# Two graph layers on one core: the second layer's probabilities turned by the transposing DMA instead of TensorE

## What is computed

```python
# layer 0
h = jnp.einsum('bnd,ade->bane', feat_in, W); th = jnp.tanh(h)
attn = attn_src + jnp.swapaxes(attn_dst, 2, 3)          # from th, leaky, masked, softmax
feat_out = jax.nn.elu(einsum(attn, h) + b)
gate = jax.nn.sigmoid(feat_in @ H_w.T + H_b)
l0 = gate * feat_out + (1.0 - gate) * feat_in
x = _layernorm(x + l0)
# layer 1: 6 heads of 128
q, k, v = _heads(x @ Wq + bq), _heads(x @ Wk + bk), _heads(x @ Wv + bv)
probs = softmax(q @ k.T / sqrt(128) + bias, axis=-1)    # 64 x 64 for each graph and head
x = _layernorm(x + (probs @ v) @ Wf + bf)
```

## Time and profile before

| | before |
|---|---|
| median of 3 runs | 2766.53 us (2765.67 to 2773.51) |
| profiled execution: its own time | 2766.33 us |
| its span, first to last instruction | 2764.6 us |
| PE busy | 99% |
| DVE, ACT, POOL busy | 60%, 42%, 39% |
| mean granted clock of PE | 0.997 |

### The profile page before, as it was taken

One profiled execution on the slowest core, in us unless ns is written; L12 is line 12 of the kernel. 1 busy time (PEld: TensorE's weight loads), 2 busy tenths in 40 slices (PEclk: granted clock), 3 DMA queues, 4 the chain that ended last, 5 costly groups with the idle time before them and its releaser, 6 DMA issues.

```text
span 2764.6 us, 51821 instructions
## 1 busy us (share of the span) xinstructions
PE 2726.9 (99%) x20988; PEld 2517.8 (91%) x20988; DVE 1668.8 (60%) x3334; ACT 1160.3 (42%) x3045; POOL 1066.3 (39%) x630
## 2 busy tenths in 40 slices
PE   8999999999999989999999999999999999999998
PEld 6877778888788889999999999999999999999998
DVE  6888998888888754444454444454445445444443
ACT  5666776666666633322332233322332233223322
POOL 2453344433444134433444343434443343434340
PEclk9999999999999999999999999999999999999999
DMA  5656665555555512222213222222222222222220
GB/s 180 173 131 145 164 160 145 139 139 139 141 137 143 175 59 69 69 71 81 70 58 81 76 75 58 79 72 71 69 68 71 81 70 58 81 81 70 58 70 23
DMA packets 306894, 269.49 MB, mean 97 GB/s; under 512 B 227808, under 2 KB 244192, under 8 KB 306656
## 3 DMA queue, kind: packets, MB, share of 16 engines
q1 hardware_dynamic: 306656, 266.19, 35.5%
HBM read 142.65 MB, written 75.89 MB: 79 GB/s over the span
## 4 chain that ended last, share of the span: by engine, by line
PE 85%; DVE 5%; DMA 4%; issue 2%; POOL 2%; ACT 2%; SPq 1%; DVEq 0%; ACTq 0%; POOLq 0%
PE ps_hg L1036 21%; PE ps_a L1199 14%; PE ps_k L70 14%; PE ps_q L70 14%; PE ps_a L70 14%; PE ps_c L1165 2%; PE ps_s L1140 2%; PE ps_pv L1068 1%; DMA dst_all<-dst_scratch 1%; ACT logits L564 1%; PE ps_t L1055 1%; PE ps_pt L1165 1%; DMA dst_scratch<-dst 1%; PE ps_pt L1147 1%; DVE logits L770 1%
## 5 line engine op out<-in xcount | busy, mean ns | idle before, releaser
L1036 PE MATMUL ps_hg<-w_hi,xT 128*128 128x512 f32 x2268 | 745.6, 401 | 8.3 <-DVE h_one L803 8.2
L1036 PEld LDWEIGHTS ps_hg<-w_hi,xT 128*128 128x128 f32 x2268 | 426.1, 188 | 112.6 <-issue 11.3
L1036 PE MATMUL ps_hg<-w_lo,xT 128*128 128x512 f32 x1134 | 448.4, 395 | 0.0
L70 PE MATMUL ps_k<-x1T_hi,wk_hi 128*128 128x256 f32 x1152 | 329.1, 286 | 0.0
L70 PE MATMUL ps_q<-x1T_hi,wq_hi 128*128 128x256 f32 x1152 | 323.5, 281 | 1.4 <-DVE x1T_lo L910 1.4
L70 PE MATMUL ps_q<-x1T_lo,wq_hi 128*128 128x256 f32 x1152 | 322.6, 280 | 0.0
L70 PE MATMUL ps_k<-x1T_lo,wk_hi 128*128 128x256 f32 x1152 | 321.9, 279 | 0.0
L70 PE MATMUL ps_q<-x1T_hi,wq_lo 128*128 128x256 f32 x1152 | 321.9, 279 | 0.0
L70 PE MATMUL ps_k<-x1T_hi,wk_lo 128*128 128x256 f32 x1152 | 321.1, 279 | 0.0
L496 POOL TENSOR_TENSOR th_src<-th,wsrc_all 128x768 f32<-128x768 f32 x64 | 118.3, 1848 | 483.7 <-DVE dst_all L783 463.4
L648 ACT ACTIVATE qT<-ps_q,bq_col 128x256 f32<-128x256 f32 x192 | 80.5, 470 | 479.3 <-PE ps_q L70 479.3
(11 more groups left out here) (144 smaller groups left out, 5814.2 us busy)
## 6 DMA issues: line engine op xcount, KB each, us to landing
x_tok<-x SPq DMA_DIRECT2D x64, 384.0 KB, 4.1
dst_all<-dst_scratch SPq DMA_DIRECT2D x128, 192.0 KB, 3.4
gate_scratch<-gate SPq DMA_DIRECT2D x64, 384.0 KB, 2.6
feat_scratch<-feat SPq DMA_DIRECT2D x128, 192.0 KB, 2.8
feat_in<-feat_scratch SPq DMA_DIRECT2D x62, 384.0 KB, 3.1
gate_in<-gate_scratch SPq DMA_DIRECT2D x62, 384.0 KB, 3.7
x_even<-x SPq DMA_DIRECT2D x16, 768.0 KB, 4.2
x_odd<-x SPq DMA_DIRECT2D x16, 768.0 KB, 4.4
```

The source lines that it names most:

```text
L70: ins = pe.matmul(out, left[a][c], right[b][c], start=(n == 0), stop=(n == len(terms) - 1))
L1036: ins = pe.matmul(ps_hg[:, cols], left[a][c], right[b][c], start=(c == 0 and n == 0), stop=(c == KC - 1 and n == 2))
```

## The change

From group 2 on PE no longer turns the probabilities. POOL splits `scores_sb` into two planes of 16 bits (`split_p1`), SP issues one transposing DMA of four 128x128 blocks (`turn_p1`), and the copies into `probs1T` now read the turned planes and join them (`join_block`). For the first two pairs ACT joins the blocks of tile 0 and DVE those of tile 1; for the third pair ACT joins all four. `scores` gets a wait for the logits of the pair before, which the transposes had implied. `scores_sb` is free for the next logits when POOL has split it. SP issues the three turns of a group after the second tile's feat and gate loads and ahead of the next group's `turn_x1`.

Besides, for all groups and for the first part too, the gate is completed on ACT (`whole_gate`, 0.5 times plus 0.5) where POOL added 1, with the constants of the mix and of its epsilon changed to suit. On DVE, `rstd_start` of the next group's input stands ahead of the third pair's logits, the second pair's joins behind them, and `rstd_end` ahead of the third `normalise`.

```diff
+        def join_block(copy, buf, t, g, signal):
+            s = graph(g)
+            out_ = probs1T[s, buf, :, s].bitcast(U16).rearrange("p (h t) (n l) -> p l h t n", t=GT, l=2)[:, :, :, t, :]
+            copy(out_, planes_p1T[t * NODES:(t + 1) * NODES, :, :, s]).then_inc(signal, 1)
...
+            def turn_p1(G, j):
+                sp.wait_ge(split_p1_done, pair_of(G, j))
+                for joined_ in (block0_done, block1_done):
+                    sp.wait_ge(joined_, 2 * (PAIRS * G + j))
+                sp.dma_start_transpose(planes_p1T.rearrange("p l h n -> p (l h) n"),
+                                       planes_p1.rearrange("p l (h m) -> p (l h) m", h=2)).then_inc(turned_p1, 16)
...
+                if G + 2 < NG:
                     sp.wait_ge(mixed, GT * (G + 2) + 1)
                     feat_and_gate(G + 2, 1)
+                if BY_DMA <= G + 1 < NG:
+                    for j in range(PAIRS):
+                        turn_p1(G + 1, j)
...
                 pool.wait_ge(delta_done, GT * G + t + 1)
-                pool.tensor_scalar(gate_, gate_, 1.0, None, ALU.add).then_inc(gate_ready, 1)
                 pool.wait_ge(gate_ready, GT * G + t + 1)
...
+            def split_p1(G, j):
+                pool.wait_ge(probs_done, PAIRS * G + j + 1)
+                if pair_of(G, j) > 1:
+                    pool.wait_ge(turned_p1, 16 * (pair_of(G, j) - 1))
+                pool.tensor_copy(planes_p1[:, :, :], scores_sb.rearrange("p k m -> p (k m)").bitcast(U16)
+                                 .rearrange("p (d l) -> p l d", l=2)).then_inc(split_p1_done, 1)
...
-                for t in range(GT):
+                for t in range(GT):
+                    if 1 <= G < NG - 1:
                         feat_less_x(G + 1, t, feat_in[:, :])
                         times_gate(G + 1, t, feat_in[:, :], gate_in[:, :])
+                    if G >= BY_DMA:
+                        split_p1(G, t)
+                if G >= BY_DMA:
+                    split_p1(G, GT)
...
+            def whole_gate(G, t, gate_):
+                if G == 0:
+                    act.wait_ge(fg_first[t], 32)
+                else:
+                    act.wait_ge(fg_in, 32 * (GT * (G - 1) + t + 1))
+                act.activation(gate_, gate_, ACT.Copy, scale=0.5, bias=0.5).then_inc(gate_ready, 1)
...
                 if G == 0:
                     for n in range(KC + 3, 2 * KC):
                         w1_round(act, EARLY_W1 + n)
+                    whole_gate(1, 1, gate_in[:, :])
...
             def scores(G, j):
+                if G >= BY_DMA:
+                    pe.wait_ge(logit_done, PAIRS * G + j)
...
-                transpose_probs1(G, 0)
+                if G < BY_DMA:
+                    transpose_probs1(G, 0)
                 scores(G, 1)
```

More of the change, by code:

```diff
@@ L195, in two_graph_layers @@
         bf_all = at(S + 55232, "bf_all", [P, D])
+        planes_p1 = at(S + 53184, "planes_p1", [P, 2, PN * NODES], U16)
+        planes_p1T = at(S + 54208, "planes_p1T", [P, 2, 2, P], U16)
         x1_tok = [x_even, x_odd]
@@ L244, in two_graph_layers @@
         turned1 = [sem(f"turned1_{t}") for t in range(GT)]
+        split_p1_done, turned_p1 = (sem(n) for n in ("split_p1_done", "turned_p1"))
         v_done, v_copied, o_done, o_added = (sem(n) for n in ("v_done", "v_copied", "o_done", "o_added"))
@@ L249, in two_graph_layers @@
             sem(n) for n in ("bias_mask", "logit_done", "max1_done", "exp1_done", "inv1_done", "probs_done"))
-        pt1_done, ptc_act, ptc_dve, c_done, c_hi, c_lo = (
-            sem(n) for n in ("pt1_done", "ptc_act", "ptc_dve", "c_done", "c_hi", "c_lo"))
+        pt1_done, block0_done, block1_done, c_done, c_hi, c_lo = (
+            sem(n) for n in ("pt1_done", "block0_done", "block1_done", "c_done", "c_hi", "c_lo"))
         biased, stat_done, mv_done, newton, norm_done = (
@@ L264, in copy_block, with pair_of @@
             copy(out_, src_).then_inc(signal, 1)
+        def join_block(copy, buf, t, g, signal):
+            s = graph(g)
+            out_ = probs1T[s, buf, :, s].bitcast(U16).rearrange("p (h t) (n l) -> p l h t n", t=GT, l=2)[:, :, :, t, :]
+            copy(out_, planes_p1T[t * NODES:(t + 1) * NODES, :, :, s]).then_inc(signal, 1)
+        def pair_of(G, j):
+            return PAIRS * (G - BY_DMA) + j + 1
         def turn_of(G, t):
@@ L629, in _ @@
                     elu_exp(T - 2)
+                for t in range(GT):
+                    if T == MIX + 2 * t:
+                        whole_gate(0, t, gate_first[:, t, :])
                 if PREFETCH < T <= PREFETCH + EARLY_W1 - LATE_W1:
@@ L677, in probs_out @@
             def probs_out(G, j):
-                act.wait_ge(pt1_done, PAIRS * G + j + 1)
-                for g in range(2):
-                    copy_block(act.copy, (G + j) % 2, 0, g, ptc_act)
+                if G < BY_DMA:
+                    act.wait_ge(pt1_done, PAIRS * G + j + 1)
+                    for g in range(2):
+                        copy_block(act.copy, (G + j) % 2, 0, g, block0_done)
+                else:
+                    act.wait_ge(turned_p1, 16 * pair_of(G, j))
+                    for g in range(2):
+                        join_block(act.copy, (G + j) % 2, 0, g, block0_done)
+                    if j == PAIRS - 1:
+                        for g in range(2):
+                            join_block(act.copy, (G + j) % 2, 1, g, block1_done)
             def context_hi(G, j):
@@ L708, in _ @@
                     k_out(G, 0)
+                    if G + 1 < NG:
+                        whole_gate(G + 1, 0, gate_in[:, :])
                 q_out(G, 1)
                 exps(G, 0)
+                if G == 0:
+                    whole_gate(1, 0, gate_in[:, :])
                 k_out(G, 1)
                 q_out(G, 2)
+                if 1 <= G < NG - 1:
+                    whole_gate(G + 1, 1, gate_in[:, :])
                 if G == 0:
@@ L724, in _ @@
                 value_out(G, 0)
-                probs_out(G, 1)
+                if G < BY_DMA:
+                    probs_out(G, 1)
                 exps(G, 2)
+                if G >= BY_DMA:
+                    probs_out(G, 1)
                 value_out(G, 1)
@@ L895, in _ @@
                     input_moments(0)
-                    rstd_start(in_newton, 0, 4 * EPS)
+                    rstd_start(in_newton, 0, EPS)
                 elif T == MIX + 2 * GT + 2:
@@ L916, in logits_of @@
                     dve.wait_ge(bias_mask, G + 1)
+                elif G < BY_DMA:
+                    dve.wait_ge(pt1_done, PAIRS * G + j)
                 else:
-                    dve.wait_ge(pt1_done, PAIRS * G + j)
+                    dve.wait_ge(split_p1_done, pair_of(G, j - 1))
                 dve.scalar_tensor_tensor(
@@ L934, in probs_out @@
             def probs_out(G, j):
-                dve.wait_ge(pt1_done, PAIRS * G + j + 1)
-                for g in range(2):
-                    copy_block(dve.tensor_copy, (G + j) % 2, 1, g, ptc_dve)
+                if G < BY_DMA:
+                    dve.wait_ge(pt1_done, PAIRS * G + j + 1)
+                    for g in range(2):
+                        copy_block(dve.tensor_copy, (G + j) % 2, 1, g, block1_done)
+                else:
+                    dve.wait_ge(turned_p1, 16 * pair_of(G, j))
+                    for g in range(2):
+                        join_block(dve.tensor_copy, (G + j) % 2, 1, g, block1_done)
             def context_lo(G, j):
@@ L975, in _ @@
                     input_moments(G + 1)
-                probs_out(G, 1)
+                    if G >= BY_DMA:
+                        rstd_start(in_newton, G + 1, EPS)
+                if G < BY_DMA:
+                    probs_out(G, 1)
                 logits_of(G, 2)
-                if 1 <= G < NG - 1:
-                    rstd_start(in_newton, G + 1, 4 * EPS)
+                if G >= BY_DMA:
+                    probs_out(G, 1)
+                elif G >= 1:
+                    rstd_start(in_newton, G + 1, EPS)
+                if BY_DMA <= G < NG - 1:
+                    rstd_end(in_newton, G + 1)
                 normalise(G, 2)
@@ L983, in _ @@
                     input_moments(1)
-                    rstd_start(in_newton, 1, 4 * EPS)
+                    rstd_start(in_newton, 1, EPS)
+                if G < BY_DMA:
+                    rstd_end(in_newton, G + 1)
                 if G + 1 < NG:
-                    rstd_end(in_newton, G + 1)
                     input_norm(G + 1)
                 context_lo(G, 0)
-                probs_out(G, 2)
+                if G < BY_DMA:
+                    probs_out(G, 2)
                 if G == 0:
@@ L1168, in probs_copied @@
             def probs_copied(G, j):
-                pe.wait_ge(ptc_act, 2 * (PAIRS * G + j + 1))
-                pe.wait_ge(ptc_dve, 2 * (PAIRS * G + j + 1))
+                pe.wait_ge(block0_done, 2 * (PAIRS * G + j + 1))
+                pe.wait_ge(block1_done, 2 * (PAIRS * G + j + 1))
             def first_context(G):
```

(6 more changed lines are left out.)

3 lines of the change are left out of this document (1 added, 2 removed).

## The result

The changed kernel is slower: median 2783.94 us (2780.21 to 2785.95, 6 runs) against 2767.48 us (6 runs), ratio 1.0051, 95% interval 1.0040 to 1.0061. The forecast was 2752 us, 2747 to 2762. The profiled execution took 2785.95 us, its span is 2784.2 us.

What follows compares the result with a forecast made beforehand. PE, busy 99% of the span, was taken to bound the kernel: 2766.33 - 17.7 saved by PE + 3.3 lost in group 0 = 2751.9, forecast 2752 us, range 2747 to 2762; the new chain was to cost nothing.

Steps and rivals of the forecast that it cites:

- what PE saves: PE without transposes in groups 2 to 31: 0.59 us less a group, 17.7 us in all, bounds 13.5 and 22.8.
- group 0: Gate completed on ACT behind three casts delays group 1's normalised x, which PE awaits: +3.3 us, bounds 0 and 3.6.
- the turn, by itself: Transposing DMA of four probability blocks: lands in 3.0 us, between 2.2 and 4.0.
- The 5.2 us: Turn of four blocks, if the skill's 1309 ns by DMA added up one after another: an estimated 5.2 us.
- a pair of joins ... I take 0.84: Copies joining a pair's turned planes into `probs1T`: 0.84 us, from ACT passes of 256 elements.
- they can be about 1 us later than before: Second pair's logits on DVE, behind the first pair's joins: about 1 us later than before.
- the very mechanism, for `normalise`: First pair's normalise on DVE meets POOL's product over the shared port: up to 0.6 us more.
- the prediction's chain: DVE, POOL, DMA and joins up to the third pair: ready at 1897.0 to 1898.6, PE asks at 1899.9, 1.3 us left.
- the split: POOL's split of `scores_sb` into two planes: about 0.6 us with its start.
- ACT's four joins: Third pair's four joins on ACT: 1.6 us.
- the place of the slack: Third pair taken as the tight one: its blocks ready 1.3 us before PE asks, 0.3 with slow turn and chain.
- The rival on the other side: Third pair late in every group through split, turn and four joins in a row: 27 us, 2779 us; chance 0.07.

Runs made afterwards that it cites:

- experiment 7: Kernel before the change, with only the gate completed on ACT and probabilities still turned by TensorE: 2765.34 us, ratio 0.9991.
- experiment 9: Changed kernel, but SP issues a group's first turn ahead of the second tile's feat and gate loads: 2751.93 us, ratio 0.9942.
- experiment 6: Changed kernel, but POOL waits for DVE's join of the first pair before subtracting x from the second tile's feat: 2755.02 us, ratio 0.9959.
- experiment 1: Changed kernel, but DVE computes the second pair's logits before joining the first pair's blocks: 2754.32 us, ratio 0.995.
- experiment 2: Changed kernel, but ACT joins all four blocks of the first pair and DVE none: 2754.01 us, ratio 0.9951.
- kernel 5: Changed kernel with DVE's second-pair logits ahead of its first-pair joins, and group 0's second gate ahead of ACT's casts: 2750.84 us, ratio 0.9941.

## Why the prediction was wrong

**Right: what PE saves.** I put 0.59 us a group and 17.7 us; measured 0.66 and 19.8. The difference may be the third pair, whose transposes may cost more than their starts; no run tests it.

**Right in its mechanism, unsettled in size: group 0.** PE's wait for `x_odd` rose by 3.6 us as worked out. The term was +3.3 us; group 0 got longer by 0.8 to 3.1 (experiment 7), and experiment 7 shows the gate part as a whole at -1.3 us (0 to -5 by its interval). In it is some 1.8 us of lost time of late groups, which went.

**Right: the turn, by itself.** I took 3.0 us; four blocks land in 2.4 (median of 90), with 4.0 still that of twelve:

```profile
DMA to landing us min/median/max: 2.4/2.4/7.0
```

The upper end is that of the first turns, which go behind the loads: they take 4.0 us in the median, and only ahead of the loads (experiment 9) 2.4. The place still came out: the first turn lands 23.4 us after the start of the group shown, where I put 22.0 to 23.5. The 5.2 us, estimated from the 1309 ns that the Trainium skill (VectorE: DVE Perf Modes, the three transpose paths) gives for one 128x128 block by DMA, are not borne out as a sum of blocks.

**Wrong: the step "a pair of joins ... I take 0.84", and with it "they can be about 1 us later than before".** For the first pair on DVE the joins take 3.5 us (median), and the second pair's logits start 3.8 us later than before. The estimate came from ACT's passes and ACT's old copies, which read PSUM; the new copies have SBUF on both sides, and on DVE they stand at the time of POOL's subtraction and product. Two paragraphs below that step the prediction tells of the very mechanism, for `normalise`, and draws on the Trainium skill (SBUF — State Buffer) for operations with two SBUF inputs. In the section "Who interferes with whom" the Trainium skill names a second kind as well, DVE copies that run in a mode with both ports; no view shows the mode, but the trace agrees in what it does to the 64x256 copies of 16 bit words (0.31 us alone, 2.0 at the longest). I had applied one half of the rule to one instruction, and never asked it of the copies the change adds. By its rule the copies and POOL's operations exclude each other, which is what experiment 6 takes apart. On from there the prediction's chain is off in its own terms: it has the second pair's normalise end at 26.7 to 27.3 us of the group, and the median is 29.8; it has the third pair's joins end at 39.0 to 40.6 us, and the median is 42.4, where it has PE ask at 41.9. With the first joins out of the way (experiments 1, 2, 5, 6 and 9) they end at 40.9 to 41.0. Two smaller terms were short too: the split, put at 0.6 us, takes 1.0 to 1.3 nearly always, and ACT's four joins, put at 1.6, take 2.0.

**Wrong: the place of the slack.** I looked at the third pair's blocks. Only 1.6 us of PE's listed waits are for those. Most of the delay went another way, through ACT's program order: late logits of the second pair hold ACT at its exponentials, and behind these stand the third pair's `k_out` (14.7 us of waits of PE in 8 of the groups) and the copies of values (5.2 us). The list understates waits, since a record of PE (0.28 us for a 128x256 product) runs on after the next could have started (0.12 us from start to start). Counted from start to start, groups 2 to 30 of the changed kernel take 34.4 us more than those of kernel 5: 16.3 of it up to the end of the third pair's scores, 10.3 from there through the first contexts and the product behind them, 6.6 in the last contexts, where the third pair's blocks are needed, 2.4 in the output products, and -1.2 in the parts ahead. The prediction listed what is queued behind DVE's joins but not what is queued behind ACT's exponentials. ACT in the group that starts at 1356.2 us, whose second gate landed 4.9 us behind the median:

```profile
1383.61 0.85 ACT L646 ACTIVATE gate_in<-gate_in 128x768 f32<-128x768 f32 x1 [4.45 <-DMA gate_in<-gate_scratch]
1384.36 0.98 ACT L272 COPY probs1T<-planes_p1T 64x256 uint16<-64x256 uint16 x2
1389.94 0.81 ACT L691 ACTIVATE kT<-ps_k,bk_col 128x256 f32<-128x256 f32 x2
```

k was ready at about 1383.3 and is copied at 1389.94; PE's row has the wait:

```profile
1390.90 0.74 PE L1219 MATMUL ps_s<-kT,qT 128*64 128x64 f32 x16 [4.46 <-ACT kT L691]
```

Late loads were there before as well: in four groups the second gate landed 1.4 to 2.1 us behind the median, and these four lost 1.9 us together. The hold-up used up the slack in every group, and what was late on top of it was paid by PE.

**The rival on the other side** had the right sign and only a small part of the place (the 6.6 us in the last contexts), and its chance of 0.07 was too small: a chain over four engines under a busy PE had one undisturbed path in my reckoning, and each of its steps could meet another engine.

## What to carry to other kernels

When work leaves a full engine for a chain over idle ones, write down for each new instruction what runs on the other engines at that minute of the period, and ask of each pair whether the two can run together: a busy share of 37% did not say that POOL was in the way at the one moment that counted. Where an engine's program is in order, ask also what stands behind an instruction that may wait, for the engine that waits for it and for the next one. And a hold-up is taken away in several ways at equal gain: another order on the held engine, another engine, another time for the transfer, or a wait that keeps the two apart.

## What the runs showed of the hardware

In the splits, POOL is held up by DVE as well, and which of the two pays goes by who starts first. The split of `scores_sb` (128x512), which I had put at 0.6 us, is 1.27 us in the median of 90. In the group of 1528.94 DVE's mix, with two SBUF inputs, starts at 1558.70 and takes 0.95 us; the split starts at 1558.85 and takes 1.28. In the group of 1356.2 the split is first:

```profile
1374.68 0.60 POOL L549 COPY planes_p<-scores_sb 128x512 uint16<-128x512 uint16 x1
```

```profile
1374.77 1.33 DVE L904 SCALAR_TENSOR_TENSOR x_even<-x_even,feat_in 128x768 f32<-128x768 f32 x1 [1.74 <-POOL feat_in L505]
```

Now the split is 0.68 us shorter and the mix 0.38 longer. Of the 58 splits that meet a mix, 53 start 0.14 us behind it and take 1.27 us; 5 start 0.09 us ahead of it and take 0.61, and then the mix takes 1.33. So a hold-up of this kind can change sides with a start that moves by 0.2 us.

PE's granted clock fell to half, 1.2 GHz, after the longest wait. The windows of that stretch (PE, PEld, DVE, ACT and POOL busy with instructions, granted clock, DMA share, GB/s):

```profile
1391.40:1394.80 3.40, 3.40 (x17) 3.28 (x13) 3.02 (x14) 0.00 (x0) 0.64 (x1) 0.50 0.19 39
1394.80:1398.20 3.40, 3.40 (x22) 3.40 (x21) 3.06 (x12) 2.66 (x11) 0.34 (x1) 1.00 0.00 0
```

In the first of them PE's value matmuls start 0.32 us apart, in the second 0.17. That is 1.5 us more for this wait of 4.46, and the changed kernel has two more such stretches of 3.4 us, in the same part of two other groups (at 2241.3 and 2524.6 us); the kernel before has none between the start of group 1 and its last 5 us. The three stretches are some 4.5 us of the 38, of which the listed waits in groups 1 to 31 make only 21.5 (14.7, 5.2 and 1.6).
